# The second bank of transposes of the feed-forward rows, moved behind the last group of value products

## What is computed

```python
def attn(X, W_Q, W_K, W_V):
    Q = _xpos(X @ W_Q)
    K = _xpos(X @ W_K, downscale=True)
    V = X @ W_V
    scores = jnp.einsum('bqd,bkd->bqk', Q, K)
    p_attn = jax.nn.softmax(scores, axis=-1)
    p_attn = p_attn * D[None, :, :]            # D = 0.9 ** |n - m|
    return jnp.einsum('bqk,bkv->bqv', p_attn, V)

def ffn(x, w_gate, w_up, w_down):              # fp4_linear rounds x and w
    gate = fp4_linear(x, w_gate)
    y = fp4_linear(x, w_up)
    h = jax.nn.silu(gate) * y
    return fp4_linear(h, w_down)

x = x + attn(_layernorm(x), W_Q, W_K, W_V)
x = x + ffn(_layernorm(x), w_gate, w_up, w_down)
```

## Time and profile before

| | us |
|---|---|
| median of 3 runs | 2570.81 |
| lowest and highest | 2567.68, 2571.44 |
| the profiled execution, its own time | 2572.08 |
| its span in the profile | 2570.3 |

### The profile page before, as it was taken

The page is one execution under the profiler, slowest core; times in us unless marked ns, Lnnn a source line. Parts: engine busy times, 40 slices in busy tenths (PEclk is TensorE's granted clock), DMA queues, the critical chain, the costliest instruction groups (busy, mean ns, idle before and its releaser), DMA issues.

```text
span 2570.3 us, 51983 instructions
## 1 busy us (share of the span) xinstructions
PE 2535.4 (99%) x16188; PEld 2293.8 (89%) x16188; DVE 2148.3 (84%) x4784; ACT 1505.4 (59%) x2966; POOL 1819.8 (71%) x1919
## 2 busy tenths in 40 slices
PE   9999989999999999999999999999999999999998
PEld 8888879999999999989999899989999999989997
DVE  8999868888888888788888888888888888888886
ACT  5666555566656655656555665566566656565654
POOL 6999947667766767667766766667766776667665
PEclk9999999999999999999999999999999999999999
DMA  8777510113111311131111311131113111221110
GB/s 286 278 282 283 192 55 23 44 34 109 40 46 30 110 42 46 32 106 44 34 42 53 98 32 46 36 108 38 46 32 106 44 42 34 78 74 40 38 38 22
DMA packets 163474, 203.29 MB, mean 79 GB/s; under 512 B 15184, under 2 KB 116752, under 8 KB 163216
## 3 DMA queue, kind: packets, MB, share of 16 engines
q1 hardware_dynamic: 163216, 200.01, 24.0%
HBM read 103.42 MB, written 77.59 MB: 70 GB/s over the span
## 4 chain that ended last, share of the span: by engine, by line
PE 81%; DMA 1%; issue 1%; SPq 1%; DVE 1%; POOL 1%; ACT 1%; DVEq 0%; ACTq 0%; POOLq 0%
PE score L483 26%; PE acc L615 19%; PE ring L483 18%; PE acc L483 8%; PE ring L583 6%; PE ring L635 3%; DMA keys<-k_dram 1%; PE ring L574 1%; PE acc L657 1%; SPq L414 1%; ACT probs L783 0%; POOL h_buf L962 0%; POOL h_buf L956 0%; POOL hq_buf L969 0%; DVE h_buf L1250 0%
## 5 line engine op out<-in xcount | busy, mean ns | idle before, releaser
L483 PE MATMUL score<-keys,q_st 128*128 128x512 f32 x3072 | 761.3, 396 | 7.1 <-ACT probs L783 3.4
L483 PEld LDWEIGHTS score<-keys,q_st 128*128 128x128 f32 x3072 | 559.6, 189 | 117.3 <-issue 3.8
L615 PE MATMUL acc<-vals,pT 128*128 128x256 f32 x3984 | 557.1, 287 | 0.8 <-DVE pT L1154 0.8
L941 POOL TENSOR_TENSOR probs<-probs,decay 128x512 f32<-128x512 f32 (+3 forms) x416 | 446.9, 1087 | 144.4 <-ACT probs L783 144.4
L483 PE MATMUL ring<-w_gu,xqT 128*128 128x512 f32 (+1 forms) x2304 | 509.1, 374 | 0.0
L615 PEld LDWEIGHTS acc<-vals,pT 128*128 128x128 f32 x3984 | 499.2, 189 | 6.1 <-DVE pT L1154 2.0
L483 PEld LDWEIGHTS ring<-w_gu,xqT 128*128 128x128 f32 x2304 | 418.6, 188 | 63.2
L753 ACT ACTIVATE pT<-ring 128x512 fp32r<-128x512 f32 (+3 forms) x432 | 226.9, 535 | 380.2 <-PE ring L583 372.7
L1167 DVE TENSOR_REDUCE smax<-score 128x1 f32<-128x1024 f32 x256 | 312.4, 1220 | 105.7 <-PE score L483 104.8
L1154 DVE TENSOR_TENSOR pT<-ring,pT 128x512 fp32r<-128x512 f32 (+3 forms) x432 | 251.0, 606 | 69.0 <-ACT pT L753 67.9
L947 POOL TENSOR_TENSOR xv<-xv,xe 128x256 f32<-128x256 f32 x128 | 94.4, 738 | 274.0 <-DVE xv L1023 274.0
(11 more groups left out here) (132 smaller groups left out, 4619.9 us busy)
## 6 DMA issues: line engine op xcount, KB each, us to landing
k_dram<-keys SPq DMA_DIRECT2D x56, 512.0 KB, 4.7
keys<-k_dram SPq DMA_DIRECT2D x56, 512.0 KB, 7.5
edge<-vals SPq DMA_DIRECT2D x288, 64.0 KB, 2.1
q_raw<-q_dram SPq DMA_DIRECT2D x129, 128.0 KB, 2.6
x_in<-X SPq DMA_DIRECT2D x32, 512.0 KB, 4.5
q_dram<-q_stage SPq DMA_DIRECT2D x32, 512.0 KB, 5.6
x_res<-X SPq DMA_DIRECT2D x128, 128.0 KB, 2.1
out<-x_res SPq DMA_DIRECT2D x128, 128.0 KB, 1.7
```

Of the source, the lines that this page charges most:

```text
L483: mm = pe.matmul(dst, stat(a, k), mov(m, k), start=i == 0, stop=ends and i == n - 1)
L615: mm = pe.matmul(pv_out, pT[g % 2][:, a, j * P:(j + 1) * P], edge[place][:] if kb in edges else vals[m][:, kb, :], start=i == 0, stop=i == ...
L941: op = pool.tensor_tensor(probs[:, k0:k1], probs[:, k0:k1], decay[:, off + k0:off + k1], ALU.mult)
```

## The change

`h_place` gives the group behind which bank h of the transposes comes, for n groups. Bank 0 stays: behind group n-3. Bank 1 was behind group n-2 and is now behind group n-1, the last. For a step without `attend` (the last four) the place is 0 as before.

```diff
+def h_place(n, h):
+
+    return max(n - 1, 0) if h else max(n - LATER, 0)
+
 def plan_slots():
...
             for h in range(2):
-                if g == min(max(len(gs) - LATER, 0) + h, max(len(gs), 1) - 1) and has(s - LAG):
+                if g == h_place(len(gs), h) and has(s - LAG):
                     take("hT", s - LAG, h)
...
                     for h in range(2):
-                        if g == min(max(len(gs) - LATER, 0) + h, len(gs) - 1):
+                        if g == h_place(len(gs), h):
                             later(h)
```

## The result

The changed kernel takes 2629.65 us (median of 4 runs, 2627.80 to 2631.31); the kernel before, run beside it, 2571.12 us. The ratio is 1.0225, with a 95% interval of 1.0211 to 1.0238: slower, by 54 to 61 us. The profiled execution took 2627.8 us, 55.7 more than the profiled one of before. The forecast was 2635, slower.

What follows compares the result with a forecast made beforehand. PE, busy 99% of the span, was taken as the bound. Terms of 50 + 5 + 7 + 2.4 us made 64 to 65 us, giving 2635 us against the median 2570.8; the range was 2600 to 2656.

Steps and rivals of the forecast that it cites:

- the two zeros for PE: On PE: the transposes' new place costs 0, and the third gate piece's wait for their bank is 0.
- The shift d: On ACT and DVE: work behind bank 1's copy comes one group of products later, 1.28 us for 11 products.
- Term 1: PE's waits for each tile's first value products, by shift plus 0.05 us less slack: nine tiles, 5.0 us a batch.
- term 2: PE's waits within a step, at the last group and down product: 0.9 us a batch, 0.33 for tile 14.
- the term that I had set to 0: DVE operations moved out of POOL's way could win back up to 0.77 us a step; taken as 0.
- the rival in which the shift is absorbed: DVE's work shortens enough to hide the delay: not slower, 2574 or 2571 us; chance 0.05 for within 0.2%.
- waits do not pass on: PE's waits for first value products stay in their step, since each step's chain starts anew with its transposes.
- Term 3: PE's restart behind a stop: 0.10 us for each of 13 stops, 1.3 us a batch.
- Term 4: Next batch's keys, queued on SP behind a store awaiting DVE: about 1.0 us a batch, 7 us in all.
- Term 5: At the kernel's end: 1.39 us at the last tile's products and 1.05 in the step after, 2.4 us.
- The rival with the clock: PE's clock falls after new stops: 2649 us if at tile 7, over 2800 if at all 13; chance 0.05.
- what would show it: Expected profile signs: PE's first-group waits 75 to 100 times, 40 to 50 us; busy near 2535, clock 1.00.

Runs made afterwards that it cites:

- e1: Changed kernel with ACT's exponentials ahead of its copy of bank 1 and DVE's three operations on h ahead of its own; 2572.99 us.
- e4: Changed kernel with bank 1 moved only in the steps of tiles 1, 3, 7, 10, 12 and 14 of each batch; 2576.16 us.
- e3: Changed kernel with DVE's three operations on h ahead of bank 1's lower half, ACT's order unchanged; 2634.54 us.
- e7: Kernel before with ACT's exponentials and DVE's three operations ahead of bank 1's copies, and SP's store behind the key loads; 2571.8 us.
- e6: Changed kernel with SP's store of tile 9 put behind the next batch's key loads; 2620.06 us.
- e8: Kernel before with SP's store of tile 9 put behind the next batch's key loads; 2568.95 us.
- e2: Changed kernel with ACT's exponentials ahead of its copy of bank 1, DVE's order unchanged; 2736.89 us.
- e9: e2 with DVE's residual and its statistics ahead of the three operations on h; 2581.17 us.

## Why the prediction was right

**The bound and the two zeros for PE** hold: PE was the bound, and the moved pair costs nothing by itself (e1, and the six moved pairs of e4). The third gate piece does not wait for bank 1 in the changed kernel; it does only where DVE copies bank 1 behind its operations on h, in e1, e3 and e7 (4.4, 4.4 and 3.1 us).

**The shift d** is as forecast: 1.29 us more idle time before ACT's copy in the step shown, handed on undiminished. Its carrier is ACT's queue (e3 against e1).

**Term 1** was forecast at 5.0 us a batch, 5.9 with its nine restarts. For tiles 3 to 12 rule and table differ by at most 0.1 us. Tiles 0 and 1 were mis-sized: with term 2's waits 0.72 and 0.91 forecast, 0.32 and 0.34 measured. Two things failed for tile 1, whose first products waited some 0.1 us instead of 0.45. One is the term that I had set to 0, DVE's work becoming shorter as it moves against POOL: in tile 0's step L1224 takes 0.50 us instead of 0.70. L1021 is shorter too, 0.57 us instead of 0.77 beside the end of POOL's `q_st`, but that gains nothing, since DVE then waits for the silu so much longer (0.76 us idle instead of 0.56). The other is that term 1 left out PE's own delay behind the transposes: between its transposes and the end of tile 0's step PE loses 0.19 us of its own, most of it around the down product, and so finds DVE that much less late. The same delay, about 0.1 us, made the waits of tiles 6, 7, 9 and 10 shorter, and in the sum the delay itself made that up. In tile 0's own step the wait for the last group did not come (term 2, 0.16 us and a restart). DVE's timeline (start, length), the operation on the scales of x in that step after (its line is L1229 there), then before:

```profile
1477.81 0.50 DVE L1229 TENSOR_SCALAR xs<-xam,rstd 128x16 f32<-128x16 f32 x1
```
```profile
1451.88 0.70 DVE L1224 TENSOR_SCALAR xs<-xam,rstd 128x16 f32<-128x16 f32 x1
```

So the rival in which the shift is absorbed was at work in one of sixteen steps, with 0.2 us. The prediction's sentence that waits do not pass on holds for PE, but e4 shows a shift that passed on to DVE's next step through POOL. And its two prices for 0.77 us a step do not agree: the term set to 0 has a lower end of 25 us, the rival of the absorbed shift 3 us for the same gain. No run decides between them.

**Term 2** (0.33 for tile 14) came to less: that step grew by 0.27, of which 0.13 is a short stop with its restart at the first group, where I had expected none. **Term 3** holds: where PE stopped, the products behind it took 0.09 to 0.12 us longer. Terms 1 to 3 together: 7.2 us a batch forecast, 7.4 - 1.1 = 6.3 measured in the fifth.

**Term 4**, 7 us: 7.0 by step lengths, 5.9 of it by the store's place (e6, e8). That the sum fits is in part luck, as the single changes of batch grew by 0.2 to 1.8 us. **Term 5**, 2.4 us, came to 2.1: the last tile's first stop went from 2.18 to 3.36 us (forecast 1.39), and from its products to the end it takes 40.6 us instead of 39.7. The second stop, in the step after, grew by 1.03 us (forecast 1.05). After, then before:

```profile
2585.39 0.80 PE L620 MATMUL acc<-edge,pT 128*128 128x256 f32 x2 [3.36 <-DVE pT L1159]
2600.94 0.69 PE L579 MATMUL ring<-ident,xq 128*128 128x128 f32 x2 [4.24 <-POOL xq L956]
```
```profile
2545.57 0.69 PE L574 MATMUL ring<-ident,xq 128*128 128x128 f32 x2 [3.21 <-POOL xq L951]
```

**The sum** was 64 us against 55.7 in the profiled executions. Some 8 of the 9 too many are terms 1 to 3 at tiles 0, 1 and 14 of the last seven batches (2.06 us a batch forecast, 0.94 measured on average); tiles 2 to 13 sum to 5.2 us a batch as forecast. The first batch grew by 3.5 us instead of 5.

**The clock** did not fall between 340 and 2585 us; the longest stop there was 1.48 us, for keys, and 0.99 us in the steps without keys. At the end it did: 3.4 us at 0.50 around the end of the stop of 3.36 us, and 6.8 us around the end of that of 4.24 us, where the kernel before had 3.4 us around its stop of 3.21. The gate's products behind that stop took 5.40 us instead of 4.80, a price that term 5 did not have. The rival with the clock is out, and the rule of the Trainium skill (TensorE: Matmul & The Clock Gate, "A second HAM failure mode: psum-queue depth-cycling"), by which frequent short idle times let the clock go back and forth, is not borne out for stops of this size, even in e2 with 123 of up to 1.3 us (its window of the steady part, granted clock 1.00):

```profile
500.00:2500.00 2000.00, 1896.72 (x12008) 1682.39 (x12007) 1655.84 (x3482) 1090.24 (x2142) 1301.48 (x1491) 1.00 0.17 52
```

**Wrong in "what would show it"**: I expected 40 to 50 us of waits in 75 to 100 places and PE's busy time unchanged; it was 26.9 us in 53 places, and 25.6 us more busy. Short stops are booked as busy time.

## What to carry to other kernels

When a unit of work moves on the busiest engine, look at what is queued behind its consumers, not only at the work itself: here 0.2 us of transposes moved by 1.3 us and took the exponentials, a table load and the silu of the next 10 us along. A slack table for each repeated step (when is the result needed, when is it there) forecast the lengths of 12 of 16 steps within 0.1 us; an average over the steps would have shown DVE 16% idle and no danger. And a DMA queue that waits in order for a result is such a consumer too.

## What the runs showed of the hardware

DVE's durations depend on which of POOL's instructions they meet, more than I had allowed for. A tensor-scalar operation on 128x704 took 521 ns in the changed kernel and 1056 beside the decay products (e2), and moving a group of small operations between the two brought it back to 544 while POOL's small ones grew from 0.55 and 0.19 to 0.95 and 0.86 us (e9). e9 is 156 us faster than e2, and DVE's order is all that differs; how much of that is the overlap with POOL, and how much that the residual no longer stands behind three operations, was not separated. In e2, 115 of the 128 operations L1023 on h began while a decay product (L948) ran on POOL. They took from 0.52 to 1.63 us, but every one of them ended 0.38 to 0.39 us after that decay product: DVE's operation is held until POOL's has ended. This agrees with the Trainium skill (SBUF — State Buffer, section "SBUF: two separate sides"), where the pair of ports that the two share is locked for a whole instruction by the one that starts first.
